# A gated attention and expert kernel on one core: tile 0's Toeplitz loaded from padded input and split on chip, with tile 0's other steps moved between the engines

## What is computed

```python
# attention: per head, all products k_i * v_j along the length, convolved causally
# with the head's kernel, plus D times themselves, then summed against q
kv  = einsum('bhil,bhjl->bijhl', k_, v_)
y   = irfft(rfft(kv, 2 * L) * rfft(ssm_kernel, 2 * L))[..., :L]
out = y + kv * D[None, None, None, :, None]
out = einsum('bijhl,bhil->bjhl', out, q_)

x = x + tanh(g_xattn[0]) * attention(ctx, ctx, layernorm(x), ssm_kernel, D)
# experts: softmax gate over 16, the best two of each row, and one shared network
x = x + tanh(g_ffn[0]) * (routed_swiglu(layernorm(x)) + shared_swiglu(layernorm(x)))
```

## Time and profile before

| | |
|---|---|
| median of 3 runs | 742.87 us (742.52 to 745.36) |
| span of the profiled execution | 739.8 us |
| PE busy | 717.1 us, 97% |
| DVE, ACT, POOL busy | 568.5, 459.4, 363.4 us |
| chain that ended last, share of the span | PE 69%, DVE 13%, DMA 6%, issue 5% |
| first work of PE | at 10.65 us |

### The profile page before, as it was taken

How to read it: one execution, slowest core, us unless ns; L and a number is a source line. 1 busy time by engine, 2 the same in 40 slices (tenths; PEclk the granted TensorE clock), 3 DMA queues, 4 the chain that set the end, 5 groups by cost and what they waited for, 6 DMA issues and landing times.

```text
span 739.8 us, 15553 instructions
## 1 busy us (share of the span) xinstructions
PE 717.1 (97%) x4602; PEld 676.3 (91%) x4602; DVE 568.5 (77%) x1111; ACT 459.4 (62%) x659; POOL 363.4 (49%) x190
## 2 busy tenths in 40 slices
PE   3999999999999999999999999999999999999998
PEld 3999999999998999899989999988989999999997
DVE  7899999999965578428899588848987699679942
ACT  6575757575432222126878588847885789578931
POOL 4999888887401065042435433543634354434320
PEclk9999999999999999999999999999999999999999
DMA  6678687877522122463667577766565764432101
GB/s 231 215 239 288 218 272 216 279 218 253 186 85 60 29 43 29 144 197 90 161 201 218 131 232 210 198 176 168 145 182 160 176 193 90 74 68 46 30 1 57
DMA packets 48404, 114.88 MB, mean 155 GB/s; under 512 B 7472, under 2 KB 8624, under 8 KB 48336
## 3 DMA queue, kind: packets, MB, share of 16 engines
q1 hardware_dynamic: 35792, 89.67, 37.1%
q0 software_dynamic: 12544, 24.40, 17.9%
HBM read 157.78 MB, written 29.26 MB: 253 GB/s over the span
## 4 chain that ended last, share of the span: by engine, by line
PE 69%; DVE 13%; DMA 6%; issue 5%; ACT 3%; SPq 1%; ACTq 1%; POOL 1%; DVEq 1%; POOLq 0%
PE pair L1303 19%; PE bank L1303 15%; PE pair L1328 12%; PE pair L1234 8%; PE bank L1328 6%; PE bank L1185 4%; PE pair L1311 3%; DMA out<-ys,slot_info 3%; DMA raw<-in_weights 2%; PE bank L1245 2%; DVE prod L829 2%; DVE bank L834 2%; DVE x L800 2%; DVE w_lo L1150 1%; DVE rows L841 1%
## 5 line engine op out<-in xcount | busy, mean ns | idle before, releaser
L1150 DVE TENSOR_TENSOR w_lo<-raw,w_hi 128x1408 fp32r<-128x1408 f32 x94 | 148.5, 1621 | 47.0 <-ACT w_hi L733 47.0
L1441 POOL DMA_INDIRECT out<-ys,slot_info x47 | 80.6, 1714 | 120.6 <-ACT ys L721 87.3
L1428 POOL DMA_INDIRECT tn<-t_rows,slot_info x47 | 75.5, 1605 | 123.1 <-DVE tT_lo L888 90.6
L733 ACT ACTIVATE w_hi<-raw 128x1408 fp32r x94 | 124.6, 1374 | 2.1 <-issue 1.4
L1234 PE MATMUL pair<-kv_hi,toep_hi 128*128 128x288 f32 x320 | 100.6, 314 | 1.7 <-DMA toep_lo<-kpad_lo 1.4
L1234 PE MATMUL pair<-kv_lo,toep_hi 128*128 128x288 f32 x320 | 95.3, 298 | 0.0
L1234 PE MATMUL pair<-kv_hi,toep_lo 128*128 128x288 f32 x320 | 95.1, 297 | 0.0
L1155 DVE TENSOR_TENSOR w_lo<-raw,w_hi 128x1536 fp32r<-128x1536 f32 x47 | 82.3, 1752 | 4.5 <-ACT w_hi L740 4.5
L1379 POOL TENSOR_TENSOR kv_lo<-kv,kv_hi 128x2304 fp32r<-128x2304 f32 x15 | 77.3, 5153 | 5.9 <-ACT kv_hi L625 5.9
L740 ACT ACTIVATE w_hi<-raw 128x1536 fp32r x47 | 69.3, 1474 | 0.1
L829 DVE TENSOR_TENSOR prod<-pair,q 128x256 f32<-128x256 f32 x128 | 53.4, 417 | 15.1 <-PE pair L1234 9.6
(11 more groups left out here) (223 smaller groups left out, 2009.3 us busy)
## 6 DMA issues: line engine op xcount, KB each, us to landing
raw<-in_weights SPq DMA_DIRECT2D x94, 704.0 KB
raw<-in_weights SPq DMA_DIRECT2D x47, 768.0 KB
toep_hi<-kpad_hi SPq DMA_DIRECT2D x15, 512.0 KB, 4.6
toep_lo<-kpad_lo SPq DMA_DIRECT2D x15, 512.0 KB, 6.2
cx<-in_ctx SPq DMA_DIRECT2D x15, 384.0 KB, 6.3
stage<-in_weights SPq DMA_DIRECT2D x16, 272.0 KB, 6.7
xt<-in_x SPq DMA_DIRECT2D x16, 256.0 KB, 6.4
xr<-in_x SPq DMA_DIRECT2D x16, 256.0 KB, 6.6
```

The costliest lines, as they stand in the source:

```text
L733: act.activation(w_hi[s % 2][:, a:b], raw[:, bass.ds(half + a, b - a)], ACT.Copy).then_inc(hi_ok[n_], 1)
L1150: dve.tensor_tensor(w_lo[s % 2][:, a:b], raw[:, bass.ds(half + a, b - a)], w_hi[s % 2][:, a:b].bitcast(F32), ALU.subtract).then_inc(lo_ok[ ...
L1428: pool.indirect_dma_start(out=tn[o % 3][:], out_offset=None, in_=t_rows, in_offset=bass.IndirectOffsetOnAxis(ap=slot_info[:, 3 * i:3 * i + ...
L1441: pool.indirect_dma_start(out=out, out_offset=bass.IndirectOffsetOnAxis(ap=rows, axis=0), in_=ys[o % 2][:], in_offset=None, bounds_check=R ...
```

## The change

For tile 0 the Toeplitz no longer goes by device memory. The host pads the kernel's rows; SP loads the shifted rows of tile 0 straight into `toep_raw`, in two pieces, and `krow` whole. POOL makes `anti`, a matrix with ones where lag 0 stands, DVE adds D there for both heads, and the split is made on chip: the high parts on ACT (`first_toep_hi`), the low part of lag block 0 on DVE, that of lag blocks 1 to 3 on POOL. The padded rows in device memory, which the other tiles still read, are made later: DVE splits `krow` after tile 0's first two blocks of kv, and SP writes both halves behind its first loads. The first piece of context and x of tile 0 are issued by ACT's queue. Tile 0's mean and variance come from DVE's `stats`, with a root on ACT and two instructions of one column on DVE. POOL forms the products of tile 0's blocks 2 and 3, and DVE those of block 1 apart. The tanh of the gates moves behind tile 1's squares on ACT. PE turns q after block 0 of tile 0, not ahead of it. In the turns of the tiles ACT does `split_kv_hi`, `split_shared`, `std_x` in this order (before: for tile 0 `std_x`, `split_kv_hi`, `split_shared`; for the others `split_shared`, `split_kv_hi`, `std_x`), and POOL `split_kv`, `form`, `split_shared` (before: for tile 0 `form`, `split_kv`, `split_shared`; for the others `form`, `split_shared`, `split_kv`).

The diff, cut to its core:

```diff
@@ SP
-            sp.dma_start(krow[:, P - 1:P - 1 + L], conv_rows).then_inc(kpad_in, 16)
+            raw_t = bass.AP(conv_rows.tensor, 0, [[1, P], [640, 2], [1, L]])
+            raw_v = toep_raw[:].rearrange("p (h c) -> p h c", h=2)
+            sp.dma_start(raw_v[:, :, 0:P], raw_t[:, :, 0:P]).then_inc(toep_raw_in[0], 16)
+            sp.dma_start(d_both[:], bass.AP(conv_d.tensor, 0, [[0, P], [1, 2]])).then_inc(d_in, 16)
+            sp.dma_start(raw_v[:, :, P:], raw_t[:, :, P:]).then_inc(toep_raw_in[1], 16)
+            sp.dma_start(cx[0][:, 2 * GW:], ctx_ext[0][:, 2 * GW:]).then_inc(ctx_in[0], 16)
+            sp.dma_start(krow[:], conv_rows).then_inc(kpad_in, 16)
             sp.dma_start(drow[:], conv_d).then_inc(kpad_in, 16)
             sp.dma_start(gts[:], gates).then_inc(gates_in, 16)
-            sp.dma_start(cx[0][:, 0:2 * GW], ctx_ext[0][:, 0:2 * GW]).then_inc(ctx_first, 16)
-            sp.dma_start(xt[0][:], x_t[0]).then_inc(x_in[0], 16)
-            sp.dma_start(cx[0][:, 2 * GW:], ctx_ext[0][:, 2 * GW:]).then_inc(ctx_in[0], 16)
...
             load(At(1), "ctx")
-            sp.wait_ge(kpadh_out, 16)
-            sp.wait_ge(kpadl_out, 16)
-            for a, b, landed in ((0, P, toep_first), (P, L, toep_in[0])):
-                for part, rows in ((toep_hi, toeplitz[0]), (toep_lo, toeplitz[1])):
-                    sp.dma_start(part[0][:].bitcast(F32).rearrange("p (h c) -> p h c", h=2)[:, :, a:b],
-                                 rows[0][:, :, a:b]).then_inc(landed, 16)
             load(At(1), "x")
+            sp.wait_ge(krowh_ok, 1)
+            sp.dma_start(kpad[0], krow_hi[:].bitcast(F32)).then_inc(kpadh_out, 16)
+            sp.wait_ge(krowl_ok, 1)
+            sp.dma_start(kpad[1], krow_lo[:].bitcast(F32)).then_inc(kpadl_out, 16)
             sp.wait_ge(kv_first, 2)
+            sp.wait_ge(kv_second, 2)
...
             load(At(2), "ctx")
+            sp.wait_ge(kpadh_out, 16)
+            sp.wait_ge(kpadl_out, 16)
             load(At(1), "toep")
@@ ACT
+            def first_toep_hi(a, b):
+                src, dst = (w[:].rearrange("p (h c) -> p h c", h=2)[:, :, a:b] for w in (toep_raw, toep_hi[0]))
+                act.activation(dst, src, ACT.Copy).then_inc(toeph_ok, 1)
...
             def turn(t):
                 first, last = t.within(0, 1), t.within(TILES - 1, TILES)
-                if first:
-                    std_x(t + 1)
+                if not last:
                     split_kv_hi(t + 1)
                 split_shared(t)
-                if not first and not last:
-                    split_kv_hi(t + 1)
+                if not last:
                     std_x(t + 1)
@@ DVE
+            dve.wait_ge(toep_raw_in[0], 16)
+            dve.wait_ge(d_in, 16)
+            dve.wait_ge(anti_ok, 2)
+            for h in range(2):
+                lag0 = toep_raw[:, h * L:h * L + P]
+                dve.scalar_tensor_tensor(lag0, anti[:], d_both[:, h:h + 1], lag0, ALU.mult, ALU.add).then_inc(toepd_ok, 1)
+            dve.wait_ge(x_in[0], 16)
+            dve.wait_ge(setup_dve, 2)
+            stats(xt, st2, mv1, stat1, At(0))
...
+            dve.wait_ge(ctx_in[0], 16)
+            pair_rows(dve, 0, 2, 2, kv_second)
...
                 products(t, 0)
+                if first:
+                    dve.wait_ge(kvh_ok, 1)
+                    first_kv_lo(2, BLOCKS, kvl_ok)
+                    dve.wait_ge(gate_tanh, 1)
@@ PE
-                                pe.wait_ge(toep_first, 32)
+                                pe.wait_ge(toepl_first, 1)
...
-                            pe.wait_ge(toep_in[0], 32)
+                            pe.wait_ge(toepl_ok, 1)
...
-            turn_q(At(0))
...
                 conv(t, 0)
+                if first:
+                    turn_q(t)
@@ POOL
-            pool.wait_ge(kv_ok, 2)
+            pool.wait_ge(ctx_in[0], 16)
+            pair_rows(pool, 0, 4, BLOCKS * 2 - 4, kv_ok)
+            pool.wait_ge(toeph_ok, 2)
+            rest, rest_hi, rest_lo = (w[:].rearrange("p (h c) -> p h c", h=2)[:, :, P:]
+                                      for w in (toep_raw, toep_hi[0], toep_lo[0]))
+            pool.tensor_tensor(rest_lo, rest, rest_hi.bitcast(F32), ALU.subtract).then_inc(toepl_ok, 1)
             form(pool, At(1))
@@ host
-        "in_conv": a("L0_xattn_ssm_kernel"),
+        "in_conv": np.pad(a("L0_xattn_ssm_kernel"), ((0, 0), (P - 1, 640 - L - (P - 1)))),
```

More of the change, by code:

```diff
@@ L222, in program @@
         drow = sb("drow", [HEADS, 1], F32, one)
+        anti = sb("anti", [P, P], F32, one)
+        anti_of = sb("anti_of", [P, P], F32, one)
+        d_both = sb("d_both", [P, 2], F32, one)
+        toep_raw = sb("toep_raw", [P, 2 * L], F32, one)
         one.close()
@@ L565, in _ @@
         def _(act):
-            act.wait_ge(gates_in, 16)
-            act.activation(small[:, 1:3], gts[:], ACT.Tanh).then_inc(gate_tanh, 1)
-            act.wait_ge(setup_dve, 3)
+            act.dma_start(cx[0][:, 0:2 * GW], ctx_ext[0][:, 0:2 * GW]).then_inc(ctx_first, 16)
+            act.dma_start(xt[0][:], x_t[0]).then_inc(x_in[0], 16)
+            act.wait_ge(setup_dve, 1)
             act.activation(small[:, 3:4], small[:, 0:1], ACT.Sqrt)
@@ L656, in _ @@
             first_kv_hi(0, 1, kvh_first)
+            act.wait_ge(toepd_ok, 2)
+            first_toep_hi(0, P)
+            act.wait_ge(stat1, 2)
+            act.activation(sd1[0][:, 0:1], mv1[0][:, 1:2], ACT.Sqrt, bias=small[:, 0:1]).then_inc(std1, 1)
             act.wait_ge(ctx_in[0], 16)
             square_rows(0, 2, BLOCKS * 2 - 2, square_ok)
-            std_x(At(0))
+            act.wait_ge(toep_raw_in[1], 16)
+            first_toep_hi(P, L)
+            norm_x(At(0))
             act.wait_ge(square_ok, 1)
+            act.wait_ge(kv_second, 2)
+            first_kv_hi(1, 2, kvh_second)
             act.wait_ge(kv_ok, 2)
-            first_kv_hi(1, 2, kvh_first)
-            norm_x(At(0))
             first_kv_hi(2, BLOCKS, kvh_ok)
+            q_copy(At(0))
             square(At(1))
-            q_copy(At(0))
+            act.wait_ge(gates_in, 16)
+            act.activation(small[:, 1:3], gts[:], ACT.Tanh).then_inc(gate_tanh, 1)
+            act.activation(small[:, 3:4], small[:, 0:1], ACT.Sqrt)
             def turn(t):
                 first, last = t.within(0, 1), t.within(TILES - 1, TILES)
-                if first:
-                    std_x(t + 1)
+                if not last:
                     split_kv_hi(t + 1)
                 split_shared(t)
-                if not first and not last:
-                    split_kv_hi(t + 1)
+                if not last:
                     std_x(t + 1)
```

54 lines of the change are left out of this document (28 added, 26 removed).

## The result

| | before | after |
|---|---|---|
| median of 6 runs, us | 743.01 (737.78 to 745.36) | 752.15 (747.17 to 755.67) |
| ratio to before | | 1.0123, 95% interval 1.0087 to 1.0159 |
| span of the profiled execution | 739.8 | 752.2 |
| last convolution matmul of the first phase, at | 207.81 | 217.75 |

What follows compares the result with a forecast made beforehand. PE was taken to bound the kernel, busy 158.29 of 160 us, with DVE right ahead of it early. 6.6 us late plus 0.5 for the clock, 7.1 on the span of 739.8, gave a median of 750.0 us, range 743.3 to 753.

Steps and rivals of the forecast that it cites:

- my sum: Whole kernel: 6.6 us for tile 1's block 1 plus 0.5 for the clock, 7.1 us late; chance 0.66.
- L: Landing of stage 0, for which ACT waits: 25.9 us by bytes, bounds 25.2 to 30.3.
- L late: Stage 0 takes 7.9 us to land, or a slow clock shows in full: +9 to +11, 753 us; chance 0.08.
- T: Time at which DVE has krow_lo ready, after turns with POOL: 17.0 us, 16.5 if the cast takes no turn.
- A: POOL's first instruction, products of tile 0 on 768 columns: 1.8 us, beginning at 6.35.
- C: POOL's low part of the Toeplitz's rest, 768 columns: 1.8 us.
- D: POOL's products of tile 1, asked for the moment C ends: 3.5 us, ahead of krow_lo.
- The clock: PE slowed after idling ahead of block 2 of tile 0, mostly hidden behind DVE: 0 to 1.9 us, taken as 0.5.
- POOL's new order: Later tiles, POOL splits, then forms: same work, kv_lo sooner, next products later; 0, at worst a few tenths.
- No turns: Rival: DVE and POOL don't hold each other up; krow_lo at about 11.1, +0.7, 743.6 us; chance 0.12.
- Stage 0 early: Rival: turns hold, but stage 0 lands under 22 and DVE's own queue decides: +2.8, 745.7 us; chance 0.08.
- It does what it says: Rival: no turns and stage 0 in time, so PE's gain of 4.3 us stays: 738.6 us; chance 0.06.

Runs made afterwards that it cites:

- e1: The changed kernel with SP's loads of gw, xr and stage for tiles 0 and 1 ahead of the writes of kpad: 745.95 us, ratio 1.0059.
- e2: The changed kernel with POOL's products of tile 1 held until DVE has split krow: 747.59 us, ratio 1.0075.
- e5: The changed kernel with krow and its D loaded first and DVE's split of krow ahead of tile 0's first products: 745.92 us, ratio 1.0033.
- e11: e5 with the load of the next Toeplitz ahead of that of the next stage in SP's turn: 743.73 us, ratio 1.0018.

## Why the prediction was right, point by point

**The sign and the place** were right: DVE and POOL in turns, `krow_lo` late, SP's queue, ACT waiting for stage 0 ahead of `std_x`, DVE late by the same, and the lag kept to the end of the phase. The time, 752.15, is 2.1 above the 750.0 forecast and inside the range, and two edits that each take a link of the chain away (e1, e2) gave back 6.0 and 4.15 us of the lag. The lag itself is larger than my sum, 9.94 against 7.1. It lies inside the bounds of L (5.9 to 11.0), but at the figure that I had given to "L late" (+9 to +11), with a chance of 0.08. Of the signs that I had named, `kpad_lo` (18.34), the end of ACT's wait (28.98), the product of block 2 (31.79) and the sums (42.83) all came, each later than I had put it.

**T, the time of krow_lo: 18.3, not 17.0.** Two errors of opposite sign. POOL's first products began at 8.38, not at 6.35: the rest of cx took 6.10 us to land, and my bounds, 5.5 to 7 for its arrival, were too early for a load behind three others in its queue (8.31). From there the turns took 9.9 us, not 10.7, for they fell otherwise than I had them: DVE's first product began at 8.33, just ahead of A, and so everything of DVE came one turn sooner. The subtraction of kv's block 1 met the Toeplitz's subtraction (C) and took 1.91; it was the cast that met D. So my first sign, that subtraction lasting over 3 us beside the products of tile 1, did not come. T came 1.3 late, where I had allowed 0.7 for the start of that chain.

**The cast.** I had left open whether it takes turns; it does, with 3.75 us beside POOL and 0.47 without. The Trainium skill (SBUF — State Buffer, Who interferes with whom) says that a cast may hold the port pair which DVE shares with GpSimd, and that the one which comes second is blocked for the whole instruction of the other; here the trace agrees, 3.75 against 0.47 us.

**SP's queue.** `kpad_lo` took 1.74 to land, not the 2.8 of the earlier trace rows; that made up for the late T, and stage 0 was issued at 22.31, where I had 22.4. This agreement is luck: 1.3 late, 1.1 early, and another 0.3 early in the issues from toep 1 to stage 0 (2.2 us, not 2.5).

**L, the landing of stage 0: 28.98, not 25.9.** This is the term that was mis-sized. I had priced the landing by bytes, at 3.5 us, with the rate of a full stretch; it took 6.65. The busy time by stretches, last column GB/s:

```profile
20.00:23.00 3.00, 2.44 (x10) 2.11 (x11) 3.00 (x7) 0.00 (x0) 1.16 (x1) 1.00 0.80 270
23.00:26.00 3.00, 3.00 (x17) 3.00 (x17) 0.92 (x3) 0.00 (x0) 3.00 (x1) 1.00 1.01 262
26.00:29.00 3.00, 3.00 (x26) 3.00 (x25) 0.00 (x0) 0.02 (x1) 3.00 (x2) 1.00 1.03 393
```

The full rate came only at the end, and 2.8 MB moved in these 9 us, where I had counted the 1.6 MB up to stage 0: even with all of ctx 2 (0.4 MB, issued at 18.87) that leaves some 0.8 MB of the four loads that were issued behind stage 0, at 22.98 to 24.54, and moved along with it. No run takes these away, so how much they cost stays open. The better guide stood in my own rows: in before the very same load, also behind toep 1, was issued at 12.86 and there at 20.50, 7.6 us. With that in place of 3.5 the sum gives 10.7, near the 9.8 measured; I had put the upper end of the earlier trace rows into the late case alone.

**From L on: 11.2 us, as costed (11.1).** 28.98 to 40.16, with DVE without a pause: 2.8 to the product of block 2, three steps, the residual with its statistics. So the 3.1 us by which stage 0 landed later than forecast are the whole of the difference: 6.6 forecast, 9.8 measured.

**The clock: 0.5 forecast, at most 0.2 to 0.4 seen.** DVE is 9.76 late at the product of tile 1's block 1, PE 10.13 at its sums, and 9.94 at the end. The wait was ahead of the turn of tile 1's q rather than the sums, and the slow stretch was hidden behind DVE, as argued.

**POOL's new order: 0 forecast, "at worst a few tenths".** Wrong as a statement on the order, though the result doesn't show it: alone it costs 4.5 us. I had weighed POOL's work and its own products, but not that SP waits for POOL's `shared_lo` ahead of a load on which PE depends; the step that I owed was to list each queue that the moved instruction holds up. In after the larger lag hides it (from 33.5 us to the marker no wait of PE is over 0.2 us), so that this error did not reach the total: luck.

**The rivals.** "No turns" falls with the cast and e2. "Stage 0 early" was run as e1: I had priced it at +2.8 by the marker, and it is +3.94, as T was late and kv's rest started at 19.84, not at 19.3. "It does what it says" asked for an L under 15 and `krow_lo` by 6. e1 had the first (stage 0 issued at 6.05, there in 5.2 us), e5 and e11 the second (`krow_lo` ready at 5.1, no wait of ACT for stage 0), and in none was PE's earlier start kept; in e5 and e11 because the root of tile 1 stands behind `kv_hi`, and that waits for POOL (1.76 us in e5). No run was free of turns, so that half of the rival is not tested.

## What to carry to other kernels

Work that is put beside other work is only free if the two engines don't take turns, and a small instruction on which a long queue hangs should never stand where it can be caught behind a long instruction of the other engine: do it first, or cut the other up. When an instruction is moved to the end of an engine's turn, list who waits for it and what stands behind that wait in the waiting queue; in these runs it was a load queue with one late wait ahead of an urgent load. Price the landing of a load from a row of the same load in the same place of its queue, rather than by its bytes. Two delays that cover each other don't add, so undoing one shows what it costs only as long as the other isn't the later.
